# Attention and expert start: layer 0's finish behind the score products, its output product in the turned rows' banks, turned rows copied out in halves, first expert group turned on TensorE

## The chip, the cores and the metric

One core of one Trainium2 chip runs the whole program. The metric is the device time of the program in microseconds (us), median of several runs. The profile is one execution of its own.

## The reference, cut to what matters

```python
x = L0_attn_x                                     # 4 x 2048 x 256, float32
xn = _layernorm(x)
s = _L0_attn_ref(xn, ...)    # tanh recurrence with 16 states; out = H @ Wo.T + bo; out * gate + residual
g = _silu(_L0_ffn_ref(xn, ...))
x = x + s * g
xn = _layernorm(x)
# L1 attention: for each of the 2048 positions i, over the 4 batch entries j <= i ("sequence" is the batch axis),
# 16 heads of 16 columns, softmax_one
q, k, v = (xn @ W.T + b for W, b in ...)          # 256 x 256 each
scores = einsum('ibhd,jbhd->ijbh', q, k) / 4      # causal in i, j
out = einsum('ijbh,jbhd->ibhd', softmax_one(scores, axis=1), v)
# L1 ffn: logits = xn @ wg, top 2 of 8 experts, capacity 2048 rows each;
# relu(rows @ w1[e] + b1[e]) @ w2[e] + b2[e], 256 -> 1024 -> 256, weighted by the gate and summed
x = x + out * _silu(moe(xn))
```

## The kernel before, in words

The program is a chain of stages: `prepare`, `mix` (layer 0 up to its gate and feed-forward, beside the recurrence), `recur` (a repeat of the recurrence that a flag on the chip asks for), `attend`, `experts`, `combine`. Each stage is a block with one instruction list for each engine, written out by hand; engines meet only at semaphores, and each engine takes its own list in order.

`attend` works on 16 tiles t of 128 positions x 4 batch entries. TensorE's list for tile t (L1334 to L1368) is: wait until the turned rows are in SBUF (L1336), the query product into `pY` (bias rows L1357 as matmuls, then L1361), the key product into `pX`, the logits into `pL` (L1348), layer 0's output product of tile t+2 into `pX` (`output`, L1315, behind a wait until the keys have been copied out, L1353), the value product into `pY`, the turning of tile t+1's rows into `pT` (L1325), and the turning of the logits (L1368). Query, key and value products are 16 matmul records each.

VectorE's list for tile t (`body`, L1082) begins with `layer0(t + 2)`: it multiplies layer 0's output product from PSUM with the stored gate (L1043), adds it into `x_st` (L1046), and takes mean and variance (L1051, L1059). Then come the score products, four multiplications of 1024, 768, 512 and 256 columns with both inputs in SBUF (L1090), their sums per head (L1096), the maximum (L1101), the difference (L1104), a wait for ScalarE's exponential (L1271), the sum (L1108), the reciprocal (L1111) and the weights `att` (L1114).

GpSimd (POOL) waits for `att` of tile t, then multiplies weights by values and adds the parts up (L1022, L1028: 1024, then 768 twice, 512 twice, 256 twice). After the first addition it has the four small operations that make scale and shift of tile t+3 (L981 to L989), which wait for L1059 of that tile.

ScalarE's list for tile t (L1289 to L1306) is: exponential of t, keys of t+1 out of PSUM (L1259), the logits' store, the normalisation of tile t+2 (L1235), logits and values of t+1, the turned rows of t+2 (L1259, one copy of 1024 columns), the turned logits of t+1, the queries of t+2.

After the last tile the routing runs on VectorE and TensorE (L1141 to L1212). `experts` then has 32 groups of 512 rows (8 experts of 4 groups). Gathers on POOL's queue (L1535) fetch the rows into `xg`; ScalarE makes the upper half precision part (L1733), VectorE the lower one (L1633), and SyncE turns both with four DMA transposes per group (L1499). TensorE's first layer (L1796 to L1798) has eight units of six matmuls; units 0 and 1 of the next group come ahead of the second layer (L1822 to L1824) of this one. The first expert's w1 is split by L1722 (ScalarE) and L1619 (VectorE) in the stage's start. The bias row of the first expert is a DMA on POOL's queue (L1529). `margin_exp` (L1738) is ScalarE's exponential for the gate.

Of the kernel before, what the change touches and what calls it, by code (L numbers as in the profile page):

```python
# [19 lines left out]
P = 128  # L20
# [753 lines left out]
def recur(nc, v):  # L774

    with ExitStack() as c:
# [4 lines left out]
        with nc.Block() as block:  # L781
# [39 lines left out]
def attend(nc, v):  # L821
# [10 lines left out]
    with ExitStack() as c:  # L832
# [118 lines left out]
        with nc.Block() as block:  # L951
            @block.sync
            def _(sp):
# [11 lines left out]
                sp.wait_ge(t_done, NT)  # L965
# [70 lines left out]
            def _(dve):  # L1036
# [45 lines left out]
                def body(i, u, left):  # L1082
                    t = 2 * i + u
                    if left >= 2:
                        layer0(t + 2)
# [6 lines left out]
                    last.then_inc(sm, 1)  # L1092
                    dve.wait_ge(sm, SM * t + 1)
# [131 lines left out]
            def _(act):  # L1225
# [53 lines left out]
                take(xnT, pT, t_done, t_evac, 0)  # L1279
# [5 lines left out]
                take(xnT, pT, t_done, t_evac, 1)  # L1285
# [3 lines left out]
                def body(i, u, left):  # L1289
# [11 lines left out]
                    if left >= 2:  # L1301
                        take(xnT, pT, t_done, t_evac, t + 2)
# [8 lines left out]
            def _(pe):  # L1311
                def output(t):
                    for n in range(2):
                        half = slice(2 * GRP * n, 2 * GRP * n + 2 * GRP)
                        last = pe.matmul(pX[:, 2 * n:2 * n + 2, :].rearrange("p b d -> p (b d)"),  # L1315
                                         v.h_st[half, :, :][:, t, :],
# [4 lines left out]
                def turn(t, u):  # L1321
# [4 lines left out]
                    last.then_inc(t_done, 1)  # L1326

                output(0)
                pe.wait_ge(op_ready, 1)
                output(1)  # L1330
# [3 lines left out]
                def body(i, u, left):  # L1334
                    t = 2 * i + u
                    pe.wait_ge(t_evac, t + 1)  # L1336
                    for n, (dst, done) in enumerate(((pY, q_done), (pX, k_done), (pY, v_done))):
                        if n == 0:
                            pe.wait_ge(v_evac, t + 1)
                        if n == 1:  # L1340

                            pe.wait_ge(op_ready, t + 2 if left >= 1 else t + 1)
                        if n == 2:
                            if not (isinstance(i, int) and t == 0):
                                pe.wait_ge(l_evac, t)
                            for kk in range(KD):
                                for b in range(B):
                                    last = pe.matmul(pL[GRP * b:GRP * b + GRP, 0:P], v.wgr[:, kk, :],  # L1348
                                                     xnT[:, kk, b * P:(b + 1) * P],
                                                     start=(kk == 0), stop=(kk == KD - 1))  # L1350
                            last.then_inc(l_done, 1)
                            if left >= 2:
                                pe.wait_ge(k_evac, t + 1)  # L1353
                                output(t + 2)
                            pe.wait_ge(q_evac, t + 1)
                        for m in range(2):
                            pe.matmul(dst[:, 2 * m:2 * m + 2, :], ones3[:, :], spread(bias3[:, n * D:(n + 1) * D], 2),  # L1357
                                      start=True, stop=False, skip_group_check=True)
                        for b in range(B):
                            for kk in range(KD):  # L1360
                                last = pe.matmul(dst[:, b, :], xnT[:, kk, b * P:(b + 1) * P],  # L1361
                                                 v.wqkv[:, kk, n * D:(n + 1) * D], start=False, stop=(kk == KD - 1),
                                                 skip_group_check=True)
                        last.then_inc(done, 1)
                    if left >= 1:
                        turn(t + 1, 1 - u)
# [23 lines left out]
def experts(nc, v):  # L1390
# [4 lines left out]
    with ExitStack() as c:  # L1395
# [35 lines left out]
        h_hi = sb("e_h_hi", [P, HT, W], F16)  # L1431
        h_lo = v.free[:, 0:HT * W // 2].bitcast(F16).rearrange("p (h w) -> p h w", h=HT)
# [5 lines left out]
        pY = psum("e_pY", [P, BLK, D])  # L1438

        passed = sem("e_passed")  # L1440
        w1_in, w2_in = v.w1_in, v.w2_in
# [38 lines left out]
        with nc.Block() as block:  # L1480
            @block.sync
            def _(sp):
# [37 lines left out]
                for n in range(2):  # L1520
                    turn(n, n, reused=False)
# [5 lines left out]
            def _(pool):  # L1527

                pool.dma_start(b2b[0], v.eb2[0].partition_broadcast(P)).then_inc(y_out[1], 16)  # L1529
# [9 lines left out]
                for n in range(3):  # L1539
# [21 lines left out]
            def _(dve):  # L1561
# [68 lines left out]
                def x_lower(n):  # L1630
                    dve.wait_ge(x_hi_ready, n + 1)
# [13 lines left out]

                dve.memset(xg[:, :, D + E:], 0.0)
                take_icol(0, 0)
# [254 lines left out]
```

## Time and profile before

| what | value |
|---|---|
| median of 3 runs | 1365.91 us (1365.15 to 1366.03) |
| profiled execution, its own time | 1364.27 us |
| its span, first to last instruction | 1362.5 us |
| busy: PE, DVE, ACT, POOL | 1159.2 (85%), 1003.9 (74%), 623.6 (46%), 613.1 (45%) us |
| mean granted TensorE clock | 0.938 of full |
| attention tiles | first score products at 293.17, last `att` (L1114) ends at 544.3 us |
| experts | first w1 matmul at 624.97, last about 1315 us |

PE is TensorE's matmuls, PEld its weight loads, DVE VectorE, ACT ScalarE, SP SyncE. A row of the timeline begins with its start and its duration in us; the bracket at its end is the time that the engine stood idle before it and what ended that. Rows of one line that follow each other are merged ("x4"). A row of a window table has its bounds, its length, then busy time and count for each engine, then the clock, the share of the DMA engines and GB/s.

### The profile page before, as it was taken

To read this page: it belongs to the slowest core of one execution; us is meant where nothing else is said; L and a number is where in the kernel's file an instruction comes from. 1 tells how busy PE (TensorE), PEld (TensorE's weight loads), DVE (VectorE), ACT (ScalarE), POOL (GpSimd) and SP (SyncE) were. 2 spreads that over 40 slices of the span, in tenths; PEclk is the share of its full clock that TensorE was granted. 3 is DMA by queue.
4 is the path that set the end of the run, shared out by engine and by line. 5 is a ranking of instruction groups with operands and counts; after the bars stand their busy time and mean duration, and the time that the engine had idled before them with its cause. 6 is when DMAs were issued, how large, how long until landed. Compare 5 with 4: busy or idle time off the path is not lost. (4 is left out here: it accounts for less than half of the span.)

```text
span 1362.5 us, 20386 instructions
## 1 busy us (share of the span) xinstructions
PE 1159.2 (85%) x7448; PEld 793.8 (58%) x7448; DVE 1003.9 (74%) x1931; ACT 623.6 (46%) x955; POOL 613.1 (45%) x526
## 2 busy tenths in 40 slices
PE   3799999689989996146999999999999999999920
PEld 3665665267666765133676666766766666667610
DVE  7777777758888889985767677676686766776538
ACT  4865655333443333004545455454455454554422
POOL 5600000028778887213555545645546455463310
PEclk9999999889999998557999999999999999999965
DMA  8170000001111112004645455555555545454259
GB/s 343 61 249 1 1 1 0 1 32 48 33 33 33 33 33 78 1 20 106 118 110 104 83 109 105 114 108 77 113 99 117 111 74 123 90 82 70 32 157 351
DMA packets 142708, 117.61 MB, mean 86 GB/s; under 512 B 83824, under 2 KB 127728, under 8 KB 142480
## 3 DMA queue, kind: packets, MB, share of 16 engines
q1 hardware_dynamic: 109248, 80.75, 19.8%
q0 software_dynamic: 24624, 34.23, 15.9%
q10 hardware_dynamic: 8736, 1.33, 0.5%
q8 instruction: 59, 0.97, 0.3%
q14 instruction: 41, 0.34, 0.1%
HBM read 55.19 MB, written 44.30 MB: 73 GB/s over the span
## 5 line engine op out<-in xcount | busy, mean ns | idle before, releaser
L1758 ACT ACTIVATE e_h_all<-e_pH,e_b1c,e_h_scale 128x512 f32<-128x512 f32 x256 | 199.6, 780 | 258.0 <-PE e_pY L1824 205.5
L1822 PE MATMUL e_pY<-e_w_hi,e_h_hi 128*128 128x256 f16 x1024 | 279.3, 273 | 2.6 <-DVE late L1669 2.6
L1823 PE MATMUL e_pY<-e_w_lo,e_h_hi 128*128 128x256 f16 x1024 | 279.1, 273 | 0.0
L1824 PE MATMUL e_pY<-e_w_hi,late 128*128 128x256 f16 x1024 | 279.1, 273 | 0.0
L1551 POOL DMA_INDIRECT expert_sums<-late,e_dcol x128 | 212.9, 1664 | 103.6 <-DVE late L1709 71.4
L1535 POOL DMA_INDIRECT e_xg<-xn_rows,e_icol x128 | 147.1, 1149 | 240.0 <-DVE e_icol L1567 153.2
L1796 PE MATMUL e_pH<-e_xT,e_w_hi 128*128 128x512 f16 x512 | 194.9, 381 | 15.6 <-DMA e_xT<-e_xs 15.6
L1669 DVE TENSOR_TENSOR late<-e_h_all,e_h_hi 128x512 f16<-128x512 f32 x256 | 177.3, 692 | 36.8 <-ACT e_h_hi L1758 31.1
L1797 PE MATMUL e_pH<-e_xT,e_w_hi 128*128 128x512 f16 x512 | 194.8, 380 | 0.0
L1798 PE MATMUL e_pH<-e_xT,e_w_lo 128*128 128x512 f16 x512 | 194.8, 380 | 0.0
L1705 DVE SCALAR_TENSOR_TENSOR late<-e_pY,e_y_scale,logit_st 128x512 f32<-128x512 f32 x64 | 48.0, 751 | 104.6 <-PE e_pY L1824 100.8
L1361 PE MATMUL c_pY<-late,c_xnT 128*128 128x256 f32 x512 | 117.7, 384 | 0.0
L1822 PEld LDWEIGHTS e_pY<-e_w_hi,e_h_hi 128*128 128x128 f16 x1024 | 100.2, 98 | 19.8 <-DVE late L1669 4.9
L1823 PEld LDWEIGHTS e_pY<-e_w_lo,e_h_hi 128*128 128x128 f16 x1024 | 100.2, 98 | 14.9
L1361 PEld LDWEIGHTS c_pY<-late,c_xnT 128*128 128x128 f32 x512 | 98.8, 193 | 17.0 <-issue 0.3
L1824 PEld LDWEIGHTS e_pY<-e_w_hi,late 128*128 128x128 f16 x1024 | 100.2, 98 | 11.6
L1758 ACT ACTIVATE e_h_hi<-e_pH,e_b1c,e_h_scale 128x512 f16<-128x512 f32 x128 | 99.1, 774 | 0.0
L1796 PEld LDWEIGHTS e_pH<-e_xT,e_w_hi 128*128 128x128 f16 x512 | 50.3, 98 | 73.2 <-DMA e_xT<-e_xs 15.6
L976 POOL MEMSET c_mhalf<- 128x4 f32 x1 | 0.1, 102 | 204.5 <-POOLq L781 204.5
L1798 PEld LDWEIGHTS e_pH<-e_xT,e_w_lo 128*128 128x128 f16 x512 | 50.3, 98 | 60.9 <-issue 1.0
L1797 PEld LDWEIGHTS e_pH<-e_xT,e_w_hi 128*128 128x128 f16 x512 | 50.3, 98 | 56.7 <-issue 0.8
L1028 POOL TENSOR_TENSOR prod_st<-prod_st,c_pv 128x768 f32<-128x768 f32 (+2 forms) x48 | 68.8, 1433 | 8.6 <-POOL c_pv L1022 8.6
(251 smaller groups left out, 2130.0 us busy)
## 6 DMA issues: line engine op xcount, KB each, us to landing
shared<-expert_w SPq DMA_DIRECT2D x16, 1024.0 KB, 6.5
expert_sums<-a_zero SPq DMA_DIRECT2D x10, 1024.0 KB, 11.3
x_st<-x SPq DMA_DIRECT2D x16, 512.0 KB, 9.0
xn_rows<-shared SPq DMA_DIRECT2D x16, 512.0 KB, 3.0
f_ya<-expert_sums SPq DMA_DIRECT2D x16, 512.0 KB, 8.1
out<-x_st SPq DMA_DIRECT2D x8, 1024.0 KB, 8.8
e_xg<-xn_rows,e_icol POOLq DMA_INDIRECT x128
e_xT<-e_xs SPq DMA_TRANSPOSE x128
```

The lines of the kernel that those rows point to most:

```text
L1028: pool.tensor_tensor(o, o, part, ALU.add).then_inc(pv_step, 1)
L1361: last = pe.matmul(dst[:, b, :], xnT[:, kk, b * P:(b + 1) * P], v.wqkv[:, kk, n * D:(n + 1) * D], start=False, stop=(kk == KD - 1), skip_g ...
L1535: pool.indirect_dma_start(xg[:, q, 0:D + E], None, v.xn3_dram, bass.IndirectOffsetOnAxis(icol[u][:, q:q + 1], axis=0), bounds_check=N - 1, ...
L1551: pool.indirect_dma_start(v.y_dram, bass.IndirectOffsetOnAxis(dcol[u][:, q:q + 1], axis=0), yo[:, q, :], None, bounds_check=N + CAP - 1, o ...
L1669: dve.tensor_tensor(h_lo[:, h, :], h_all[h % 2][:, :], h_hi[:, h, :], ALU.subtract).then_inc(h_lo_ready, 1)
L1758: last = act.activation(dst, pH[h % NPH][:, :], ACT.Relu, bias=b1c[eu][:, h:h + 1], scale=h_scale[eu][:, 0:1])
L1796: pe.matmul(pH[h % NPH][:, :], w1_hi[:, k, rows], x_hi[:, k, :], start=(k == 0), stop=False)
L1797: pe.matmul(pH[h % NPH][:, :], w1_hi[:, k, rows], x_lo[:, k, :], start=False, stop=False)
L1798: last = pe.matmul(pH[h % NPH][:, :], w1_lo[:, k, rows], x_hi[:, k, :], start=False, stop=(k == KD - 1))
L1822: pe.matmul(pY[:, q, :], h_hi[:, h, cols], w2_hi[:, h, :], start=(h == 0), stop=False)
L1823: pe.matmul(pY[:, q, :], h_hi[:, h, cols], w2_lo[:, h, :], start=False, stop=False)
L1824: last = pe.matmul(pY[:, q, :], h_lo[:, h, cols], w2_hi[:, h, :], start=False, stop=(h == HT - 1))
```

## The change

It has three places. In `recur`, ScalarE's wait within the conditional repeat is one lower. In `attend`, `layer0(t + 2)` moves from the head of VectorE's tile to behind the score products; its output product moves from behind the logits to between query and key product and goes into `pT`, so the turning of the next tile's rows waits until L1043 has read it; the turned rows are copied out in two halves of 512 columns, the query product starts its first half after the first of them, and its bias matmuls are ahead of that wait. In `experts`, the gathers of the first group go ahead of the bias row's DMA, its rows are split in four parts, turned on TensorE into PSUM and copied out by ScalarE, in place of four DMA transposes; VectorE splits w1 after that; and ScalarE's `margin_exp` of a group moves one group later.

```diff
@@ recur, ScalarE
-                        act.wait_ge(summed, L * n + l + 1)
+                        act.wait_ge(summed, L * n + l)
@@ attend, VectorE
                 def layer0(t):
                     dve.wait_ge(o_done, t + 1)
-                    dve.tensor_tensor(v.prod_st[:, t, :], pX[:, :, :].rearrange("p b d -> p (b d)"),
-                                      v.prod_st[:, t, :], ALU.mult).then_inc(op_ready, 1)
+                    src = pX[:, :, :].rearrange("p b d -> p (b d)") if t < 2 else pT[:, :, :].rearrange("p k c -> p (k c)")
+                    dve.tensor_tensor(v.prod_st[:, t, :], src, v.prod_st[:, t, :], ALU.mult).then_inc(op_ready, 1)
...
                 def body(i, u, left):
                     t = 2 * i + u
-                    if left >= 2:
-                        layer0(t + 2)
                     dve.wait_ge(k_evac, t + 1)
                     dve.wait_ge(q_evac, t + 1)
...
                     last.then_inc(sm, 1)
+                    if left >= 2:
+                        layer0(t + 2)
                     dve.wait_ge(sm, SM * t + 1)
@@ attend, ScalarE (in the place of take(xnT, pT, ...))
+                def take_turned(t):
+                    for kk in range(KD):
+                        act.wait_ge(t_done, KD * t + kk + 1)
+                        act.activation(xnT[:, kk, :], pT[:, kk, :], ACT.Copy).then_inc(t_evac, 1)
@@ attend, TensorE (turn now signals t_done after each kk)
+                def product(t, n, dst, done):
+                    for m in range(2):
+                        pe.matmul(dst[:, 2 * m:2 * m + 2, :], ones3[:, :], spread(bias3[:, n * D:(n + 1) * D], 2),
+                                  start=True, stop=False, skip_group_check=True)
+                    for kk in range(KD):
+                        if n == 0:
+                            pe.wait_ge(t_evac, KD * t + kk + 1)
+                        for b in range(B):
+                            last = pe.matmul(dst[:, b, :], xnT[:, kk, b * P:(b + 1) * P], ...)
+                    last.then_inc(done, 1)
...
                 def body(i, u, left):
                     t = 2 * i + u
+                    pe.wait_ge(v_evac, t + 1)
+                    product(t, 0, pY, q_done)
+                    if left >= 2:
+                        output(t + 2, in_pT)
+                    if t == 0:
+                        pe.wait_ge(op_ready, 2)
+                    else:
+                        pe.wait_ge(k_evac, t)
+                    product(t, 1, pX, k_done)
...
+                    last.then_inc(l_done, 1)
+                    pe.wait_ge(q_evac, t + 1)
+                    product(t, 2, pY, v_done)
                     if left >= 1:
+                        if left >= 2:
+                            pe.wait_ge(op_ready, t + 3)
                         turn(t + 1, 1 - u)
@@ experts, SyncE and POOL
-                for n in range(2):
-                    turn(n, n, reused=False)
+                sp.wait_ge(first_turned, BLK)
+                turn(1, 1, reused=False)
...
-                pool.dma_start(b2b[0], v.eb2[0].partition_broadcast(P)).then_inc(y_out[1], 16)
+                pool.wait_ge(icols, 1)
+                for q in range(BLK):
+                    pool.indirect_dma_start(xg[:, q, 0:D + E], None, v.xn3_dram, ...).then_inc(first_in[q], 16)
+                pool.dma_start(b2b[0], v.eb2[0].partition_broadcast(P)).then_inc(y_out[1], 16)
+                for n in range(1, 3):
                     gather(n, n % 2)
@@ experts, VectorE
                 scales(0, 0)
-                lower_w1(0, 0)
-                x_lower(0)
+                for q in range(BLK):
+                    dve.wait_ge(first_hi, q + 1)
+                    last = dve.scalar_tensor_tensor(xs[:, q, D:2 * D], ...).then_inc(first_lo, 1)
+                dve.sem_inc(x_lo_ready, 1)
+                for q in range(BLK):
+                    dve.wait_ge(first_in[q], 16)
                 margin(0, 0, 0)
                 take_icol(1, 1)
+                lower_w1(0, 0)
                 x_lower(1)
@@ experts, ScalarE
+                act.activation(ident16, v.ident, ACT.Copy).then_inc(ident_ready, 1)
+                for q in range(BLK):
+                    act.wait_ge(first_in[q], 16)
+                    act.activation(xs[:, q, 0:D], xg[:, q, 0:D], ACT.Copy, scale=X_SCALE).then_inc(first_hi, 1)
                 upper_w1(0, 0)
-                x_upper(0, 0, 1)
+                for q in range(BLK):
+                    cols = slice(q * P, (q + 1) * P)
+                    act.wait_ge(first_turned, q + 1)
+                    act.activation(xT[0][:, :, cols], first_turn[q], ACT.Copy).then_inc(first_ready, 1)
                 margin_exp(0, 0)
                 x_upper(1, 1, 1)
-                margin_exp(1, 1)
...
-                        margin_exp(n + 2, (g + 2) % GRPS)
+                        margin_exp(n + 1, (g + 1) % GRPS)
@@ experts, TensorE
+                pe.wait_ge(ident_ready, 1)
+                for q in range(BLK):
+                    pe.wait_ge(first_lo, q + 1)
+                    for kk in range(2 * KD):
+                        last = pe.transpose(first_turn[q][:, kk, :], xs[:, q, kk * P:(kk + 1) * P], ident16)
+                    last.then_inc(first_turned, 1)
+                pe.wait_ge(first_ready, BLK)
+                pe.sem_inc(x_turned, 16 * BLK)
```

## Rows read from the trace of the kernel before

**Rows 1.** Busy time of each engine in three stretches (window table).
```profile
368.90:499.40 130.50, 116.99 (x666) 90.15 (x666) 114.73 (x185) 52.95 (x89) 104.91 (x88) 1.00 0.11 34
...
603.00:625.00 22.00, 0.98 (x4) 0.61 (x5) 10.58 (x22) 3.16 (x3) 8.92 (x9) 0.50 0.38 80
625.00:1315.00 690.00, 674.04 (x4629) 452.65 (x4629) 472.60 (x923) 343.35 (x518) 351.93 (x248) 0.99 0.51 95
```
**Rows 2.** Waits, 320 to 499 us: total, times, longest.
```profile
DVE prod_st L1043 <- PE c_pX L1315: 10.6, 11, 1.3
```
**Rows 3.** Timeline of one attention tile in the steady state, 352 to 369 us.
```profile
352.44 1.13 PE L1315 MATMUL c_pX<-late,shared 64*128 64x512 f32 x4 [0.54 <-ACT c_work L1259]
352.71 1.93 POOL L1022 TENSOR_TENSOR prod_st<-c_att,c_v 128x1024 f32<-128x1024 f32 x1 [1.70 <-DVE c_att L1114]
...
354.82 1.49 POOL L1022 TENSOR_TENSOR c_pv<-c_att,c_v 128x768 f32<-128x768 f32 x1 [0.18 <-POOL prod_st L1022]
354.87 2.52 DVE L1046 TENSOR_TENSOR x_st<-prod_st,x_st 128x1024 f32<-128x1024 f32 x1
356.49 2.58 POOL L1028 TENSOR_TENSOR prod_st<-prod_st,c_pv 128x768 f32<-128x768 f32 x1 [0.18 <-POOL c_pv L1022]
...
357.39 1.04 PE L1325 MATMUL c_pT<-cst,shared 128*128 128x128 f32 x8
...
359.50 2.99 DVE L1090 TENSOR_TENSOR c_work<-c_work 128x1024 f32<-128x1024 f32 x4
...
360.10 3.62 PE L1361 MATMUL c_pY<-late,c_xnT 128*128 128x256 f32 x16
...
362.53 3.00 DVE L1096 TENSOR_REDUCE c_sc<-c_work 128x64 f32<-128x1024 f32 x4
...
363.98 3.62 PE L1361 MATMUL c_pX<-late,c_xnT 128*128 128x256 f32 x16
...
368.69 0.42 DVE L1114 TENSOR_TENSOR c_att<-c_ex,c_mx 128x256 f32<-128x256 f32 x1
```
**Rows 4.** Timeline, tile 14: no layer 0 work is left, so score products follow `att`.
```profile
515.82 7.67 DVE L1090 TENSOR_TENSOR c_work<-c_work 128x1024 f32<-128x1024 f32 x4
...
529.69 0.42 DVE L1114 TENSOR_TENSOR c_att<-c_ex,c_mx 128x256 f32<-128x256 f32 x1
```
**Rows 5.** Timeline, tile 0 and what leads to it.
```profile
278.49 0.20 POOL L981 TENSOR_TENSOR c_ta<-c_mv,c_eps 128x4 f32<-128x4 f32 x1 [7.93 <-DVE c_mv L1059]
...
286.33 1.02 ACT L1259 ACTIVATE c_work<-c_pX 128x1024 f32<-128x1024 f32 x1 [2.86 <-PE c_pX L1361]
...
288.59 1.22 DVE L1043 TENSOR_TENSOR prod_st<-c_pX,prod_st 128x1024 f32<-128x1024 f32 x1 [10.18 <-PE c_pX L1315]
...
293.17 3.00 DVE L1090 TENSOR_TENSOR c_work<-c_work 128x1024 f32<-128x1024 f32 x4
```
**Rows 6.** Groups by line, 150 to 600 us: a 512-column copy out of PSUM.
```profile
L667 ACT ACTIVATE a_gT<-a_pGU,gconst 128x512 f32<-128x512 f32 x9 | 6.2, 687 | 6.2 <-PE a_pGU L750 6.2
```
**Rows 7.** Timeline, the start of the experts, 611 to 640 us.
```profile
611.22 2.00 ACT L1722 ACTIVATE e_w_hi<-shared,e_scale 128x2048 f16<-128x2048 f32 x1 [68.68 <-DVEq L1615]
...
616.85 15.96 SPq L1499 DMA_TRANSPOSE e_xT<-e_xs  x8
...
624.97 0.61 PE L1796 MATMUL e_pH<-e_xT,e_w_hi 128*128 128x512 f16 x1 [15.55 <-DMA e_xT<-e_xs]
...
625.16 1.06 ACT L1733 ACTIVATE e_xs<-e_xg 128x1024 f16<-128x1024 f32 x1 [7.56 <-DMA e_xg<-xn_rows,e_icol]
...
639.88 0.27 PE L1822 MATMUL e_pY<-e_w_hi,e_h_hi 128*128 128x256 f16 x1
```
**Rows 8.** TensorE at its lower clock: a query product (timeline), and a fall (window table).
```profile
276.83 5.58 PE L1361 MATMUL c_pY<-late,c_xnT 128*128 128x256 f32 x16
...
533.60:536.00 2.40, 0.03 (x1) 0.00 (x0) 2.40 (x3) 1.11 (x2) 2.22 (x2) 1.00 0.00 0
536.00:537.00 1.00, 0.00 (x0) 0.00 (x0) 1.00 (x1) 0.00 (x0) 1.00 (x1) 0.90 0.00 0
```

More of the change, by code:

```diff
@@ L1278, in _ @@
                 normalise(0, 0, 0)
-                take(xnT, pT, t_done, t_evac, 0)
+                take_turned(0)
                 normalise(1, 1, 0)
@@ L1284, in _ @@
                 take_v(0, 0, reused=False)
-                take(xnT, pT, t_done, t_evac, 1)
+                take_turned(1)
                 put_logits(0)
@@ L1301, in body @@
                     if left >= 2:
-                        take(xnT, pT, t_done, t_evac, t + 2)
+                        take_turned(t + 2)
                     if left >= 1:
@@ L1311, in _, with output @@
             def _(pe):
-                def output(t):
+                def output(t, dst):
                     for n in range(2):
                         half = slice(2 * GRP * n, 2 * GRP * n + 2 * GRP)
-                        last = pe.matmul(pX[:, 2 * n:2 * n + 2, :].rearrange("p b d -> p (b d)"),
-                                         v.h_st[half, :, :][:, t, :],
+                        last = pe.matmul(dst[n], v.h_st[half, :, :][:, t, :],
                                          v.wo_pad[half, 2 * n:2 * n + 2, :].rearrange("p b d -> p (b d)"),
@@ L1325, in turn @@
                             last = pe.transpose(pT[:, kk, b * P:(b + 1) * P], xn[u][:, b, kk * P:(kk + 1) * P], ident)
-                    last.then_inc(t_done, 1)
-                output(0)
+                        last.then_inc(t_done, 1)
+                def product(t, n, dst, done):
[6 more added lines that the diff above has]
+                        for b in range(B):
+                            last = pe.matmul(dst[:, b, :], xnT[:, kk, b * P:(b + 1) * P],
+                                             v.wqkv[:, kk, n * D:(n + 1) * D], start=False, stop=(kk == KD - 1),
+                                             skip_group_check=True)
+                    last.then_inc(done, 1)
+                in_pX = [pX[:, 2 * n:2 * n + 2, :].rearrange("p b d -> p (b d)") for n in range(2)]
+                in_pT = [pT[:, n, :] for n in range(2)]
+                output(0, in_pX)
                 pe.wait_ge(op_ready, 1)
-                output(1)
+                output(1, in_pX)
                 turn(0, 0)
@@ L1335, in body @@
                     t = 2 * i + u
[L1336 to L1358, printed above, removed]
-                        for b in range(B):
[L1360 to L1364, printed above, removed]
@@ new lines, in body @@
+                    pe.wait_ge(v_evac, t + 1)
[7 more added lines that the diff above has]
+                    product(t, 1, pX, k_done)
+                    if t:
+                        pe.wait_ge(l_evac, t)
+                    for kk in range(KD):
+                        for b in range(B):
+                            last = pe.matmul(pL[GRP * b:GRP * b + GRP, 0:P], v.wgr[:, kk, :],
+                                             xnT[:, kk, b * P:(b + 1) * P], start=(kk == 0), stop=(kk == KD - 1))
@@ L1438, in experts @@
         pY = psum("e_pY", [P, BLK, D])
+        first_turn = [pH[q][:, 0:KD * P].bitcast(F16).rearrange("p (k w) -> p k w", k=2 * KD) for q in range(BLK)]
         passed = sem("e_passed")
+        first_in = [sem(f"e_first_in{n}") for n in range(BLK)]
+        ident_ready = sem("e_ident_ready")
+        first_hi = sem("e_first_hi")
+        first_lo = sem("e_first_lo")
+        first_turned = sem("e_first_turned")
+        first_ready = sem("e_first_ready")
         w1_in, w2_in = v.w1_in, v.w2_in
@@ L1537, in gather @@
                                                 bounds_check=N - 1, oob_is_err=False).then_inc(x_in[u], 16)
-                for n in range(3):
+                pool.wait_ge(icols, 1)
+                for q in range(BLK):
+                    pool.indirect_dma_start(xg[:, q, 0:D + E], None, v.xn3_dram,
+                                            bass.IndirectOffsetOnAxis(icol[0][:, q:q + 1], axis=0),
+                                            bounds_check=N - 1, oob_is_err=False).then_inc(first_in[q], 16)
+                pool.dma_start(b2b[0], v.eb2[0].partition_broadcast(P)).then_inc(y_out[1], 16)
+                for n in range(1, 3):
                     gather(n, n % 2)
```

16 lines of the change are left out of this document (9 added, 7 removed).

## The prediction

> **What bounds the kernel now.** I read the window table first. In eight steady attention tiles (130.5 us, 16.3 each) TensorE is busy 117 us and VectorE 115, POOL 105: nobody has much room, and the period is set by a ring of all of them [rows 1]. In the experts TensorE is busy 674 of 690 us, so there only an earlier start can pay; in the 22 us before, it is busy 1 [rows 1]. The waits show what the attention part of the change goes for: VectorE stands 10.6 us in 11 tiles for layer 0's output product, about 0.97 each [rows 2], and TensorE stands 0.54 us for the keys' copy ahead of it [rows 3].
>
> The timeline of one tile shows what the sums below rest on. VectorE and POOL get in each other's way when both work out of SBUF: L1046 took 2.52 us, from 354.87 to 357.39, beside a POOL multiplication that ended at 356.31, and the POOL addition issued at 356.49 ended at 359.07, 1.68 after L1046 did [rows 3]. Alone L1046 takes what L1043 takes, 1.22. The four score products took 2.99, because in this order they meet only POOL's small operations [rows 3]. In tile 14 there is no layer 0 work left; the score products follow `att` at once, as POOL begins its three large operations, and the same four instructions took 7.67 us [rows 4]. That is the order which the change makes the rule for tiles 1 to 13.
>
> **The attention, part by part.** Let S be the start of a tile's score products and D their length. Two rings must close.
>
> VectorE's ring: D, then layer 0 work, 4.6 (288.59 to 293.17, undisturbed, since POOL then waits for its statistics [rows 5]), then sums to the end of `att`, 6.6 (362.53 to 369.11 [rows 3]): from the products' end to the end of `att` 11.2. Then a pause d until the next keys are there. Period = d + D + 11.2.
>
> TensorE's ring, new: the turning now waits for L1043, which waits for the score products. After D: L1043 1.27 with its gap; the first half turned, about 0.9 (eight transposes 1.04 plus their load [rows 3]); its copy 0.6, between half of the 1.02 for 1024 columns [rows 5] and the 0.69 of a 512-column one [rows 6]; 0.3 to the first matmul; query start to key start 3.88 (360.10 to 363.98, the keys' bias in it) [rows 3]; the output product in between 1.1 [rows 3]; key product 3.62 [rows 3]; keys' copy 1.02 with 0.03 of gap [rows 5]. Sum 12.7. Period = D + 12.7. Logits, value product and the value copy lie beside VectorE's D + 1.3 and cost nothing; if D were 3.0 they would stick out by about half a microsecond. The query bias now lies in that shadow too. The second half's copy is behind the first four matmul pairs, nothing. Normalisation, exponential and stores on ScalarE keep their order; it is free when the halves come.
>
> The two rings give d = 12.7 - 11.2 = 1.5. Now D, from the end of `att`: POOL's first product runs 0.1 to 2.0 (1.93 [rows 3]); score product 1 waits for it and ends at 3.2; POOL's second (1.49) to 4.7; product 2 to 5.6; the addition (1.68) to 7.3; products 3 and 4 to 8.2. So D = 8.2 - 1.5 = 6.7, by taking turns as in tile 14, where 2.99 + 1.93 + 1.49 + 1.68 = 8.1 stands against 7.67 measured, the last product's end tucked in; I take 6.6 [rows 3, 4]. **Period 6.6 + 12.7 = 19.3 us, against 16.3.** Lower bound: no pause, D = 7.67 and VectorE's ring alone, 18.9. Upper bound: POOL comes late. It must wait for the statistics until 4.6 after the score products and has 13.1 busy a tile [rows 1], 5.1 of it done: it would end at 12.6, 1.4 after `att`, and D would grow to 8.1, period 20.8. But its small operations are short when VectorE holds nothing: L981 took 0.20 [rows 5] where it meets score products now, so I expect it ready about when `att` is.
>
> What goes away, 0.97 of wait for the output product and about 0.7 of L1046's mean delay, is in these rings already.
>
> The Trainium skill, page "SBUF — State Buffer", section "Who interferes with whom", says that a VectorE instruction with two SBUF inputs and a GpSimd instruction that reads SBUF shut each other out for a whole instruction. By that rule the eight pieces can only follow each other, 8.1 from the end of `att`; it doesn't say who is next when one of VectorE's ends and POOL waits, and if VectorE were, the period would be that of the first rival below. The row of tile 14 speaks for turns.
>
> First tile: the keys' copy ended at 287.35 [rows 5]. The query product starts some 1.5 to 2 earlier, and the output product ahead of the keys costs about 2 at the low clock of that stretch [rows 8], so S(0) = 287.5. POOL is idle then, D = 3.0, so S(1) = 287.5 + 3.0 + 12.7 = 303.2. Thirteen periods: S(14) = 303.2 + 13 x 19.3 = 554.1, against 515.82 [rows 4]: +38.3. Tiles 14 and 15 keep their order; D there falls from 7.67 to about 6.6 in two tiles but the key chain sets most of it: -1.2. **Attention +37.1** (bounds: 18.9 gives 32, 20.8 gives 57). The copy's added fixed cost, 16 times 0.2 to 0.3, is on ScalarE, which has over half its time free [rows 1].
>
> **Recurrence.** The wait stands in a conditional; no instruction of L810 is in this trace. Zero, unless the repeat ran.
>
> **Start of the experts.** Scales are done at 611.2, when L1722 starts [rows 7]. First group new: gathers are issued from about 603.3 instead of 604.3 and land by 611; ScalarE's four small parts are done by then; VectorE's four lower parts take 1.3 to 1.7, to 612.8; TensorE turns, to 613.4; ScalarE has w1 until 613.2, then four copies of 512 columns at about 0.66, to 616.0; VectorE splits w1 until 615.8. First matmul at 616.1 instead of 624.97 [rows 7]: 8.9 earlier. But group 1 still comes by DMA: its gather starts about 3.8 earlier than before (L1567 moves ahead of the w1 split), so ScalarE's part comes at about 621.3 for 625.16, the lower part ends near 623.7, and the four transposes take what they took, 8.1 (616.85 to 624.97) [rows 7]: 631.9. TensorE needs them at about 628.5 and stands some 3 us, and ScalarE can't empty the first banks before 622.4, which is hidden behind four banks. Second layer at 634.5 for 639.88 [rows 7]. **-5.4**, kept to the end since TensorE is full from there; bounds -3 (slower transposes) and -8.9 (no stall). Dropping one DMA issue on POOL ahead of the gathers, four transposes on SyncE's queue, and the moved `margin_exp`: ScalarE isn't what TensorE waits for, nothing.
>
> **Sum.** +37.1 - 5.4 = +31.7 on the profiled execution: 1364.3 + 31.7 = 1396.0. The median of the runs is 1.6 above that execution; I predict 1397.
>
> **Rivals.**
> 1. *VectorE keeps its turn* (faster). Once it has begun, its four products run together, D = 0.5 + 3.0 = 3.5, period 16.2: the attention ends where it did, -1 with the first tile, the experts give 5.4: 1359. It decides in the four products after `att`; if D stays under about 4 the kernel is faster. Against it: 7.67 in tile 14, no reason to think that tile special [rows 4]. 8%. A milder form, D near 4.5, ends within 0.2% to 1% above; with it 2% for no change.
> 2. *TensorE's clock falls in its new gap* (slower still). From the value product's end, S + 3.8, to the turning, S + 7.9, it stands about 4.1 us. After its last matmul of the attention (to 533.63) the clock was full until 536.0 and 0.90 on the mean of the next microsecond, so it fell at about 536.8, 3.2 us on; the query product took 5.58 there for 3.62 [rows 8, 3]. The Trainium skill, page "TensorE: Matmul & The Clock Gate", section "Why this matters for your kernels", warns that such gaps between bursts send the clock back; by that rule this case would come in part of the tiles. The price is small, since a later key copy makes d longer and lets POOL finish first: with 2.2 more in TensorE's ring d is 3.7, D 4.9, period 19.8; with 4.4 more, 20.1. 13 times 0.5 to 0.8, and perhaps 2 in the expert start: 1404 to 1409. 20%.
> 3. *POOL late*, D = 8.1: period 20.8, 1397 + 19.5 = 1416. 8%.
>
> The forecast itself, 62%, has 1388 to 1403 as its own range. The whole range 1383 to 1415 leaves out rival 1, most of rival 3 and a little of each side. 0.2% (2.7 us) is about what a measurement of this kernel can tell from no change. Faster 0.09, same 0.02, slower 0.89.
>
> **What would show it.** Right: L1090's group near 6.5 us a tile in place of 3.6, L1046 at 1.23 in all tiles, `att` every 19.3 us, a TensorE wait of about 4 us for L1043 ahead of L1325, VectorE's wait for L1315 gone, a new one of 1.5 for the keys' copy. In the experts the first L1796 11.9 us or so after the first gather's index copy, then a stall of 3 on the transposes. Wrong: L1090 at 3 to 4 us, or a period under 17.

## The result, and the profile after

| | before | after |
|---|---|---|
| median of 4 runs, side by side | 1365.53 us (1364.99 to 1366.03) | 1402.72 us (1402.48 to 1404.19) |
| span of the profiled execution | 1362.5 us | 1401.0 us |
| mean granted TensorE clock | 0.938 | 0.930 |

The ratio is 1.0275, with a 95% interval of 1.0257 to 1.0292: 37 us slower. Forecast were 1397 us and a range of 1383 to 1415. The sign, the mechanism and the range held; the point was 5.7 us too low.

From the profile page of after, the busy time of each engine:

```profile
PE 1179.9 (84%) x7464; PEld 805.3 (57%) x7464; DVE 1031.3 (74%) x1934; ACT 626.4 (45%) x979; POOL 586.3 (42%) x526
```

The work is the same but for 16 more matmuls (the first group's turning, x7464 for x7448), and TensorE is busy 20.7 us longer with it: a first sign that it ran at the lower clock more often. VectorE is busy 27.4 us longer, since the time that an instruction of VectorE stands behind one of POOL counts as busy. POOL is busy 26.8 us less: its small operations for the statistics (L981 to L987), which had lain beside the score products and took 3.2 us a tile before, now take 1.4.

**Where the 38.5 us of span went.** The stages ahead of the attention end 0.46 us later. The last `att` ends at 584.77 instead of 544.31, so the attention takes 40.0 more. The routing behind it takes the same (58.68 and 58.71 from there to the first gather's index copy). From that copy to the table load of `combine`, 709.58 for 711.51: 1.9 less. 0.46 + 40.0 - 1.9 = 38.5.

The waits of after, 325 to 540 us (engine, line, released by; total, times, longest), show what the tile is made of now.

```profile
POOL c_ta L981 <- DVE c_mv L1059: 67.9, 11, 6.4
...
PE c_pT L1329 <- DVE prod_st L1044: 40.1, 11, 4.6
...
DVE c_work L1088 <- ACT c_work L1259: 23.0, 11, 2.6
```

The wait that the change went for, VectorE's 0.97 a tile for the output product [rows 2], is gone. In its place VectorE waits 2.1 a tile for the keys (L1088), and TensorE 3.6 a tile for L1044 ahead of the turning. Both are the new waits that were forecast. POOL waits 6.2 a tile for statistics, but in time: it starts each tile's first large operation 0.5 after `att` starts, as before, so rival 3 did not come.

The timeline of after over one tile and the start of the next two (start, duration; in the bracket the idle time ahead and what ended it) holds the whole ring. D is again the time of a tile's four score products.

```profile
359.37 0.42 DVE L1114 TENSOR_TENSOR c_att<-c_ex,c_mx 128x256 f32<-128x256 f32 x1
359.87 1.93 POOL L1022 TENSOR_TENSOR prod_st<-c_att,c_v 128x1024 f32<-128x1024 f32 x1 [0.89 <-DVE c_att L1114]
...
361.35 1.02 ACT L1259 ACTIVATE c_work<-c_pX 128x1024 f32<-128x1024 f32 x1 [3.34 <-PE c_pX L1340]
...
361.98 1.49 POOL L1022 TENSOR_TENSOR c_pv<-c_att,c_v 128x768 f32<-128x768 f32 x1 [0.18 <-POOL prod_st L1022]
...
362.41 5.57 DVE L1088 TENSOR_TENSOR c_work<-c_work 128x1024 f32<-128x1024 f32 x4 [2.61 <-ACT c_work L1259]
363.66 2.57 POOL L1028 TENSOR_TENSOR prod_st<-prod_st,c_pv 128x768 f32<-128x768 f32 x1 [0.18 <-POOL c_pv L1022]
...
367.90 1.21 DVE L1044 TENSOR_TENSOR prod_st<-c_pT,prod_st 128x1024 f32<-128x1024 f32 x1
369.15 1.23 DVE L1046 TENSOR_TENSOR x_st<-prod_st,x_st 128x1024 f32<-128x1024 f32 x1
...
369.17 1.09 PE L1329 MATMUL c_pT<-cst,shared 128*128 128x128 f32 x8 [3.29 <-DVE prod_st L1044]
...
370.64 3.62 PE L1340 MATMUL c_pY<-late,c_xnT 128*128 128x256 f32 x16
...
374.18 1.13 PE L1320 MATMUL c_pT<-late,shared 64*128 64x512 f32 x4
...
375.69 3.62 PE L1340 MATMUL c_pX<-late,c_xnT 128*128 128x256 f32 x16
...
379.05 0.42 DVE L1114 TENSOR_TENSOR c_att<-c_ex,c_mx 128x256 f32<-128x256 f32 x1
...
379.34 1.02 ACT L1259 ACTIVATE c_work<-c_pX 128x1024 f32<-128x1024 f32 x1 [1.66 <-PE c_pX L1340]
...
380.40 6.88 DVE L1088 TENSOR_TENSOR c_work<-c_work 128x1024 f32<-128x1024 f32 x4 [0.92 <-ACT c_work L1259]
...
388.47 1.97 PE L1329 MATMUL c_pT<-cst,shared 128*128 128x128 f32 x8 [4.60 <-DVE prod_st L1044]
...
401.01 5.95 DVE L1088 TENSOR_TENSOR c_work<-c_work 128x1024 f32<-128x1024 f32 x4 [2.24 <-ACT c_work L1259]
```

Read it from 362.41. The score products take 5.57 and 6.88 where they took 2.99 [rows 3], because POOL's three large operations lie among them. L1046 takes 1.23 where it took 2.52 [rows 3]. From the products' end (367.98) the chain L1044, turning, query product, output product, key product, copy (379.34) leads to the next products at 380.40: 12.42, where 12.7 was forecast. 12.42 and D = 6.88 make 19.30, and the next `att` does start at 398.35, 19.30 after 379.05.

The second turn of the ring differs. The turning at 388.47 took 1.97 instead of 1.09, after a wait of 4.60. The window table of after for two microseconds around it (busy time and count of PE, PEld, DVE, ACT, POOL, then the clock):

```profile
387.00:388.00 1.00, 0.00 (x0) 0.00 (x0) 1.00 (x2) 0.00 (x0) 0.00 (x0) 0.89 0.00 0
388.00:389.00 1.00, 0.53 (x3) 0.53 (x4) 0.96 (x2) 0.00 (x0) 0.00 (x0) 0.50 0.00 0
```

TensorE stood from 383.87 on, and the granted clock went from full to half, 2.4 to 1.2 GHz, at about 387.8. From the products' end (387.28) to the next ones (401.01) it is then 13.73: 1.31 more. VectorE starts its products later, meets less of POOL (D 5.95 for 6.88), and the `att` after that comes 19.67 instead of 19.30 later. So a fall costs 0.37 of period. By the starts of L1114 and L1088 in this trace, the chain took 12.42 in 4 of the 13 transitions between tiles 0 and 13 (periods 19.29 to 19.30) and 13.7 to 14.1 in the other 9 (19.67 to 19.69, one 19.86).

Two more things stand in the record of the granted clock. A tenth fall lies in tile 13, behind the last of these transitions. And the length of TensorE's wait does not decide alone: with the same 3.3 us, tiles 4, 8 and 12 kept the full clock, and tiles 7 and 11 lost it.

The start of the experts in after (timeline). "SPq" is SyncE's queue.

```profile
643.45 0.17 DVE L1590 COPY e_icol<-late 128x4 int32<-128x4 int32 x1 [0.81 <-PEq L951]
...
654.05 2.35 DVE L1642 SCALAR_TENSOR_TENSOR e_w_lo<-shared,e_scale,e_w_hi 128x2048 f16<-128x2048 f32 x1 [0.36 <-ACT e_w_hi L1751]
654.57 2.76 POOL L1552 DMA_INDIRECT e_xg<-xn_rows,e_icol  x1 [4.11 <-DVE e_icol L1590]
...
656.65 0.58 PE L1838 MATMUL e_pH<-e_xT,e_w_hi 128*128 128x512 f16 x1 [2.56 <-DVE e_w_lo L1642]
...
657.63 0.99 POOL L1552 DMA_INDIRECT e_xg<-xn_rows,e_icol  x1 [0.30 <-issue]
...
663.06 1.06 ACT L1761 ACTIVATE e_xs<-e_xg 128x1024 f16<-128x1024 f32 x1 [7.01 <-DMA e_xg<-xn_rows,e_icol]
...
665.58 5.23 SPq L1518 DMA_TRANSPOSE e_xT<-e_xs  x4
...
678.67 0.27 PE L1864 MATMUL e_pY<-e_w_hi,e_h_hi 128*128 128x256 f16 x1
```

The first w1 matmul comes 13.20 after the index copy; it came 21.95 after it before (603.02 to 624.97 [rows 7]): 8.75 earlier. The second layer begins 35.22 after the copy for 36.86: only 1.64 earlier. Between lie a wait of 1.46 for ScalarE, which was busy with group 1's upper half, and one of 3.31 for group 1's transposes, until 674.38. Behind that the clock was low once more, until about 677.9: 0.68 of full on the mean of 676 to 679 us. From the end of the wait for the transposes to the second layer it is 4.29.

### The profile page after: what moved, and what is told of

It is laid out like the page before. It is cut to its first block and busy times, and to the rows that moved or that the text cites. A ratio compares the mean times of both kernels' runs of the same rounds, so it can differ in the third digit from the quotient of the medians.

```text
span 1401.0 us, 20442 instructions
## 1 busy us (share of the span) xinstructions
PE 1179.9 (84%) x7464; PEld 805.3 (57%) x7464; DVE 1031.3 (74%) x1934; ACT 626.4 (45%) x979; POOL 586.3 (42%) x526
## 5 line engine op out<-in xcount | busy, mean ns | idle before, releaser
L1552 POOL DMA_INDIRECT e_xg<-xn_rows,e_icol x124 | 140.5, 1133 | 241.6 <-DVE e_icol L1590 141.2
L1088 DVE TENSOR_TENSOR c_work<-c_work 128x1024 f32<-128x1024 f32 (+1 forms) x64 | 96.5, 1565 | 36.0 <-ACT c_work L1259 36.0
L1340 PE MATMUL c_pY<-late,c_xnT 128*128 128x256 f32 x512 | 122.0, 393 | 0.0
L1340 PEld LDWEIGHTS c_pY<-late,c_xnT 128*128 128x128 f32 x512 | 103.1, 202 | 20.6 <-issue 2.5
```

What stands on the lines that cost most here:

```text
L1088: last = dve.tensor_tensor(qk[:, PAIR0[j]:PAIR0[j] + w, :], q[:, j:B, :], spread(k[:, j, :], w), ALU.mult)
L1552: pool.indirect_dma_start(xg[:, q, 0:D + E], None, v.xn3_dram, bass.IndirectOffsetOnAxis(icol[u][:, q:q + 1], axis=0), bounds_check=N - 1, ...
```

## The experiments

The kernel before, beside them, had medians of 1364.96 (e1 to e4) and 1364.97 us (e5 to e8).

**e1: the order undone, all else kept.**

```diff
                 def body(i, u, left):
                     t = 2 * i + u
+                    if left >= 2:
+                        layer0(t + 2)
                     dve.wait_ge(k_evac, t + 1)
...
-                    if left >= 2:
-                        layer0(t + 2)
                     dve.wait_ge(sm, SM * t + 1)
```

> The changed kernel with one thing undone: layer0(t + 2) is back ahead of the score products on VectorE. The output product in the turned rows' banks, the two halves and the new expert start stay. Theory (the score products beside POOL's three large operations are the loss): L1090's group goes back to 3.0 to 4.1 us a tile, L1044 no longer waits for its product since that is made before the keys, the turning waits for nothing, and the period is 15.0 to 15.6 us; 1350 to 1354 us in all. Rival (the wait of the turning for L1044 or the place of the output product is the loss): the period stays above 17 and the kernel above 1375.

Measured: 1352.58 us (1351.15 to 1353.06), ratio 0.9907 (0.9891 to 0.9924). Timeline of e1:

```profile
458.94 0.42 DVE L1114 TENSOR_TENSOR c_att<-c_ex,c_mx 128x256 f32<-128x256 f32 x1
...
463.98 1.81 POOL L1028 TENSOR_TENSOR prod_st<-prod_st,c_pv 128x768 f32<-128x768 f32 x1 [0.18 <-POOL c_pv L1022]
464.55 4.13 DVE L1090 TENSOR_TENSOR c_work<-c_work 128x1024 f32<-128x1024 f32 x4
...
474.87 0.42 DVE L1114 TENSOR_TENSOR c_att<-c_ex,c_mx 128x256 f32<-128x256 f32 x1
```

The period is 15.93. The products no longer wait for keys; the first of them meets the end of POOL's third operation, and they take 4.13. The bound is VectorE itself, and it is a little slower than expected. One move in VectorE's list is thus worth 50.1 us of after, and e1 is faster than both kernels: with the old order the rest of the change pays.

**e4: the order alone, in the kernel before.** The same move as in the change, and nothing else.

```diff
-                    if left >= 2:
-                        layer0(t + 2)
                     dve.wait_ge(k_evac, t + 1)
...
                     last.then_inc(sm, 1)
+                    if left >= 2:
+                        layer0(t + 2)
```

> The kernel before with only layer0(t + 2) moved behind the score products on VectorE; product into pX, whole copies and expert start as before. Theory: VectorE's ring alone, no pause for the keys, score products 7.67, period 18.9 to 19.4; 1398 to 1406 us. Rival (the loss needs the turned rows' banks to be shared): period 16.3, 1366.

Measured: 1399.37 us (1398.22 to 1399.98), ratio 1.0250 (1.0233 to 1.0267): +34.4. Timeline of e4:

```profile
455.08 0.42 DVE L1114 TENSOR_TENSOR c_att<-c_ex,c_mx 128x256 f32<-128x256 f32 x1
455.42 7.68 DVE L1088 TENSOR_TENSOR c_work<-c_work 128x1024 f32<-128x1024 f32 x4
455.58 2.84 POOL L1022 TENSOR_TENSOR prod_st<-c_att,c_v 128x1024 f32<-128x1024 f32 x1 [0.89 <-DVE c_att L1114]
...
460.78 2.05 POOL L1028 TENSOR_TENSOR prod_st<-prod_st,c_pv 128x768 f32<-128x768 f32 x1 [0.18 <-POOL c_pv L1022]
...
474.17 0.42 DVE L1114 TENSOR_TENSOR c_att<-c_ex,c_mx 128x256 f32<-128x256 f32 x1
```

and its groups by line and shape, 362 to 530 us:

```profile
L1088 DVE TENSOR_TENSOR c_work<-c_work 128x768 f32<-128x768 f32 x9 | 24.2, 2687 | 0.0
L1088 DVE TENSOR_TENSOR c_work<-c_work 128x256 f32<-128x256 f32 x9 | 18.3, 2029 | 0.0
...
L1088 DVE TENSOR_TENSOR c_work<-c_work 128x1024 f32<-128x1024 f32 x8 | 9.7, 1218 | 0.0
```

Here VectorE is first: its 1024-column product runs free in 1.22, and POOL's first large operation takes 2.84 for 1.93. Then each of the three smaller products costs 2.0 to 2.7 (the one of 512 columns 1.98), though the one of 256 columns is the smallest piece of work among them: each stands behind one POOL operation. That is taking turns, one instruction each. D is the 7.68 of tile 14 [rows 4], and no pause for keys follows, which is the lower bound of the forecast (18.9): 19.09 here. The order by itself costs nearly all that the change loses. In this trace the granted clock fell in six tiles of the attention too, and the period stayed at 19.1: where VectorE sets the ring, the fall costs nothing that shows.

**e2: the attention alone, with the expert start of before.** The function `experts` is that of the kernel before.

> The changed attention with the expert start of before. Theory: the attention costs 40 us and the expert start gives back about 2, so 1404.5 to 1405. Rival: the new expert start gives the 5 that was forecast and the attention costs more elsewhere: 1408.

Measured: 1405.73 us (1404.72 to 1406.76), ratio 1.0301 (1.0283 to 1.0318). That is 0.7 above the expected range and 2.3 below the rival. The attention costs 40.8 over before; beside the 1402.72 of after the expert start is worth 3.0. Against e4, the shared banks and TensorE's new order cost a further 6.4 once VectorE's order is moved. With the old order the same edits gain 8.8 (e1 against e5, below).

**e5: the expert start alone, in the kernel before.**

> The kernel before with the new expert start alone. Theory (read from the changed kernel's trace: first w1 matmul 8.7 us earlier against the index copy, then 3.3 us of wait for the second group's transposes and 1.7 us at the lower clock behind it, and 1.5 us until ScalarE is free): 2 us are left, 1362.5 to 1364. Rival (the start gives its 5): 1360 or less.

Measured: 1361.41 us (1360.50 to 1362.60, 8 runs), ratio 0.9975 (0.9964 to 0.9985): 3.6 faster. That is more than I expected after reading the trace of after, and less than the 5.4 of the prediction; it lies between the theory and the rival. A window of e5:

```profile
627.00:629.00 2.00, 2.00 (x6) 0.76 (x5) 1.97 (x5) 2.00 (x5) 1.50 (x2) 0.50 0.61 121
```

The clock fell a second time in e5 as well, but ahead of the stall (about 626.5 to 630) and not behind it. TensorE ran dry later, its wait for group 1's transposes is 1.77, and the second layer begins 2.60 after that wait for the 4.29 of after. Over the whole stage, index copy to table load, the traces of five kernels with this expert start (after, e1, e5, e6, e7) gave 706.9 to 709.6 us and those of before, e2 and e4 711.5 to 712.4. The first group scatters by about as much as the start is worth, so I go by the runs: 3.0 and 3.6. The scatter can be read. The transposes are there 29.9 to 30.9 us after the index copy, and the second layer begins 2.6 us later in e5, e6 and e7, but 3.9 in e1 and 4.3 in after, the two whose clock fell behind the stall.

**e3: POOL's three large operations cut to one head.**

```diff
+                        hs = slice(0, 1) if j < 2 else slice(0, H)
-                        pool.tensor_tensor(part.rearrange("p (i h d) -> p i h d", i=w, h=H), a, row,
+                        pool.tensor_tensor(part.rearrange("p (i h d) -> p i h d", i=w, h=H)[:, :, hs, :],
+                                           a[:, :, hs, :], row[:, :, hs, :],
                                            ALU.mult).then_inc(pv_step, 1)
...
+                            cs = slice(0, DK) if j == 1 else slice(0, (B - j) * D)
-                            pool.tensor_tensor(o, o, part, ALU.add).then_inc(pv_step, 1)
+                            pool.tensor_tensor(o[:, cs], o[:, cs], part[:, cs], ALU.add).then_inc(pv_step, 1)
```

> The changed kernel with POOL's first three large operations of a tile cut to one head of 16 columns per entry (the weighted values of heads 1 to 15 for the first two entries are left out). All waits stay. Theory (mutual exclusion of VectorE and POOL): the score products take 3.0 to 3.6 us, TensorE's ring closes at 12.5 + 3.1 = 15.6, the kernel takes 1346 to 1352. Rival (the new dependency of the turning on L1044 makes the period by itself): the period stays above 18 us, 1385 or more.

Measured: 1341.08 us (two runs, 1340.40 and 1341.75), ratio 0.9825 (0.9806 to 0.9845). Timeline of e3:

```profile
456.38 0.43 DVE L1116 TENSOR_TENSOR c_att<-c_ex,c_mx 128x256 f32<-128x256 f32 x1
...
456.88 0.30 POOL L1023 TENSOR_TENSOR prod_st<-c_att,c_v 128x64 f32<-128x64 f32 x1 [0.90 <-DVE c_att L1116]
...
457.73 3.05 DVE L1090 TENSOR_TENSOR c_work<-c_work 128x1024 f32<-128x1024 f32 x4 [0.93 <-ACT c_work L1261]
...
471.83 0.42 DVE L1116 TENSOR_TENSOR c_att<-c_ex,c_mx 128x256 f32<-128x256 f32 x1
```

VectorE's order is that of after, and still D is 3.05 and the period 15.45. TensorE's wait for the turning shrinks to 0.77, and the clock stays full in all these tiles. So it is not the place of layer 0's finish as such, nor TensorE's longer chain, that costs the time: it is that the score products now meet POOL's large operations. Less POOL work behind the last tile is in this time too, so it came out below the expected span of 1346 to 1352.

**e6: the gap of TensorE filled.** Twelve matmuls into a bank that nobody uses, ahead of the wait for L1044.

```diff
                         if left >= 2:
+                            for m in range(12):
+                                pe.matmul(pR[:, :], ones3[:, :], spread(bias3[:, 0:D], 2), start=True, stop=True)
                             pe.wait_ge(op_ready, t + 3)
```

> The changed kernel with twelve extra matmuls a tile (bias rows into a bank that nothing reads) in TensorE's gap ahead of its wait for L1044. Theory: the gap falls to about 1 to 2 us, the granted clock stays full in the attention, TensorE's ring is 12.4 behind the score products in every tile, the period is 19.2 to 19.3 instead of 19.6 on the mean, and the kernel takes 1397 to 1399. Rival (the clock has no price here): within 1.5 us of the changed kernel's 1402.7. A second one (extra matmuls are in the way): above 1405.

Measured: 1400.16 us (1399.37 to 1401.28), ratio 1.0261 (1.0246 to 1.0277): 2.6 less than after, outside the theory and outside both rivals; the interval overlaps that of after. Timeline of e6, one tile where the clock held and one where it did not:

```profile
467.45 1.09 PE L1329 MATMUL c_pT<-cst,shared 128*128 128x128 f32 x8 [2.02 <-DVE prod_st L1044]
...
481.99 2.75 PE L1377 MATMUL d_pR<-c_bias,c_ones 128*128 128x512 bf16 x12
...
486.76 1.97 PE L1329 MATMUL c_pT<-cst,shared 128*128 128x128 f32 x8 [2.02 <-DVE prod_st L1044]
```

Of the nine falls in the 13 transitions three are left, and the periods without one are 19.30 to 19.32, but for one of 19.95. But the total does not prove the price. Six falls less give 6 x 0.37 = 2.2; the filling made tile 0 1.6 later (its wait was only 0.75 there) and that one tile 0.6 longer; `att` of tile 13 starts at 554.97, for 554.99 in after. The tenth fall of after, in tile 13, is gone as well: VectorE no longer waits 1.26 for the keys ahead of tile 14's products, and the last `att` starts 0.9 earlier. The rest of this trace's gain lies in the expert stage (706.9 for 709.6), where the two kernels have the same code: the transposes were there 1.1 earlier, and no fall followed them. What a fall costs is better read tile by tile: 19.67 for 19.30 in after, and 19.69 for 19.31 in e6's own three. Why the clock still fell in three tiles, after waits of only 2.02, stays open.

**e7: e1 with the turned rows copied out in one piece.**

```diff
-                    for kk in range(KD):
-                        act.wait_ge(t_done, KD * t + kk + 1)
-                        act.activation(xnT[:, kk, :], pT[:, kk, :], ACT.Copy).then_inc(t_evac, 1)
+                    act.wait_ge(t_done, KD * t + KD)
+                    act.activation(xnT[:, :, :], pT[:, :, :], ACT.Copy).then_inc(t_evac, KD)
```

> The kernel with layer0's place restored (e1), and the turned rows copied out in one piece of 1024 columns instead of two halves. Theory: there VectorE's ring sets the period of 15.9 us and TensorE has room, so the halves are worth nothing: within 1.5 us of e1's 1352.6. Rival (TensorE's ring sets the period in e1): 16 tiles x 0.4 us, 1359.

Measured: 1353.62 us (1351.53 to 1356.18), ratio 0.9919 (0.9904 to 0.9934), against 0.9907 of e1. The intervals overlap: where VectorE is the bound, the halves are worth nothing that these runs can tell. In after, where TensorE's chain counts, they were not tried apart.

**e8: e1 without the early units ahead of the first second layer.** An attempt to lift the stall on group 1's transposes.

```diff
                     if g == 0:
                         pe.wait_ge(w1_lo_ready, e + 1)
                         pe.sem_inc(passed, 1)
+                    if g == 0 or n == 1:
                         first_layer(e, g, n, range(EARLY))
                     first_layer(e, g, n, range(EARLY, HT))
-                    if g < GRPS - 1:
+                    if g < GRPS - 1 and n > 0:
                         first_layer(e, g + 1, n + 1, range(EARLY))
```

> The kernel with layer0's place restored (e1), and in the first expert group alone the second layer is not preceded by two units of the next group, so TensorE doesn't stand for the second group's transposes. Theory: the wait of 3.3 us and the lower clock behind it go, the second layer's start then waits for VectorE's split of w2; 1.5 to 3 us less than e1: 1349.5 to 1351. Rival (VectorE sets the end of that stretch anyway): within 0.7 us of e1.

Measured: 1355.84 us (1354.24 to 1356.04), ratio 0.9929 (0.9915 to 0.9942): 3.3 slower than e1, where a gain was expected. The intervals of the two ratios overlap a little, so the loss is less sure than the missing gain. The theory fell. The waits of TensorE in e8, 615 to 660 us, and a window of it:

```profile
PE e_pY L1865 <- DVE e_w_lo L1649: 3.0, 3, 1.1
```

```profile
631.00:633.00 2.00, 2.00 (x11) 1.40 (x10) 0.86 (x8) 0.00 (x0) 0.51 (x1) 0.50 0.36 75
```

and of e1 after its own stall:

```profile
629.00:631.00 2.00, 2.00 (x21) 1.80 (x19) 1.86 (x7) 0.01 (x1) 0.00 (x0) 1.00 0.02 4
```

The second layer did begin earlier (622.59 for 628.00), but w2's lower half was not ready: VectorE was still splitting it, and TensorE stood three times. The clock fell and stayed at half for 6.8 us (from about 627.6 to 634.4); in e1 it was low for 3.4, until 628.9. The last piece of w2's split ends 33.1 after the index copy in e1 and in e8 alike, and e1's second layer begins only at 33.8: the stall on the transposes had hidden the split.

## Why the prediction was right, and where it was off

**The score products meet POOL's large operations: right.** D was put at 6.6, against 3.5 for rival 1. Measured: 5.57 to 6.88 in after, 3.05 in e3 without POOL's work, 7.68 in e4. By the Trainium skill, page "SBUF — State Buffer", section "Who interferes with whom", the two engines shut each other out for whole instructions; the trace agrees, with 7.81 and 8.19 from one `att`'s end to the end of the next products, beside the 8.2 of the forecast (four products and three POOL operations, so seven pieces where the prediction says eight). That VectorE doesn't keep its turn is settled by e4's shapes; rival 1 is out.

**The ring: right in its sum, off in its shares.** VectorE's part from products to `att` was put at 11.2 and is 11.49: L1104 takes 1.12 in after (0.66 before), since POOL's 256-column operations now lie beside it. It costs nothing, as TensorE's chain is the longer one and the pause d shrinks to 0.92 (forecast 1.5). TensorE's chain, put at 12.7, is 12.42; D is 6.88. 12.42 + 6.88 = 19.30, the forecast period to the digit, wherever the clock holds.

**The attention's size: the step that failed is the choice between my own case and rival 2.** I gave the clock's fall 20% and left it out of the sum. It came in 9 of 13 transitions. The ring then grew by 1.3 to 1.7, less than the 2.2 that the rival took, and the period by 0.37, less than its 0.5. The damping is as argued there: later keys let POOL finish first. In us: tile 1's products start at 302.47 for 303.2, -0.7; the 13 periods took 254.2 for 250.9, +3.3; tiles 14 and 15 gained 0.4 and not 1.2, +0.8. 37.1 - 0.7 + 3.3 + 0.8 = 40.5, the measured difference at the last `att`, of which 0.46 lies ahead of the stage. The clock accounts for both pluses, as an estimate: nine falls at 0.37 are 3.3, and the tenth, in tile 13, is worth the 0.9 by which e6 ends the attention earlier without it. The warning of the Trainium skill, page "TensorE: Matmul & The Clock Gate", section "Why this matters for your kernels", which the prediction weighed, agrees with this trace in that the falls came with the new gaps; but not every gap of that length brought one, and e6 had three after waits of 2.02. What misled me was one row, a fall 3.2 us after the last matmul of the attention [rows 8]: I took 4.1 us of gap as near that and still unlikely to matter. In after the fall came in waits of 3.3 to 4.6, and in some tiles only after the turning had begun.

**Rival 3, POOL late: did not come.** POOL had its statistics in time and was ready at `att` in every steady tile.

**Recurrence: zero, as forecast.** The routing and the stages ahead moved by less than 0.5.

**Start of the experts: right at the first matmul, mis-sized behind it.** The first w1 matmul came 13.20 after the index copy; my times (616.1 for 603.02) make it 13.1. (The "11.9" of the prediction's last part does not agree with that sum; 13.1 is the number.) The term that failed is the arrival of group 1's transposes, put at 631.9, that is 28.9 after the copy; it was 30.9 (671.07, when TensorE ran dry, plus 3.31). 1.4 of that are already in the lower part, which ended 22.05 after the copy for 20.7, and 0.7 in the transposes themselves (8.9 for 8.2). Ahead of it the first gather of group 1 took 2.76 on POOL where the next took 0.99. That is 2.0 of the miss. The other 1.7 is a second fall of the clock after the stall, which I had put at nothing: 4.29 from the transposes to the second layer, for the 2.6 of my times (634.5 - 631.9), which e5, e6 and e7 do show. The wait of 1.46 for ScalarE is a third thing that I had wrong, as I had written that four banks hide it; but it cost nothing here, since TensorE had to stand for the transposes anyway. 5.4 - 2.0 - 1.7 = 1.7. So 8.75 were won at the first matmul, 1.64 were left at the second layer, and by the runs the start is worth 3.0 to 3.6 for 5.4.

Together: +40.0 + 0.46 - 1.9 = 38.5 on the profiled execution against +31.7. The median of after lies at its profiled execution, so the 1.6 by which the median of before lay above its own was not there a second time. 1396.0 + 1.6 would be 1397.6; the point was put at 1397, 1.0 above 1396.0, and so it missed by 5.7 and not by 6.8.

**What pays.** The change as a whole loses because of one of its moves. With `layer0(t + 2)` left at the head of VectorE's tile, the rest (the output product in the turned rows' banks, the copy in halves, the new expert start) is 12.4 us faster than before.

## What to carry to other kernels

When two engines exclude each other at SBUF, an order is not only about who waits for whom by semaphore: ask which long instructions of the other engine each group will lie beside, and add the two up instead of laying them over each other. Before a wait is moved, look in the trace for a place where the new neighbourhood already exists (here the last tiles, 7.67 for 2.99) and take its price. And where a move opens a gap of several microseconds on TensorE in every tile, put the lower clock into the sum and not among the risks, at the price that the ring pays: 0.37 us a tile here where TensorE's chain closes the ring, nothing that shows in e4 where VectorE does.

## What the runs showed of the hardware that I had not expected

- The exchange at the shared SBUF access is one for one even where the pieces are very unequal: in e4 a 256-column product took 2.03 us and a 768-column one 2.69, each beside one POOL operation; alone they are around 0.4 and 0.9 (411 and 945 ns in e1). The same values come back in every tile from 3 to 13 of e4 (D 7.68 each time). That it is a fixed turn and not chance is inferred from that, and no run tests the rule of the exchange itself.
- The issue of a gather on POOL took 2.76 us (after, at 654.57) and 2.73 (e1, at 605.31) while VectorE split w1; the median of all 128 gathers is 1.03 in both traces. The trace of after repeats it: a gather was issued beside the w1 split of each of the other seven experts as well, took 2.31 to 2.32 us every time, and ended 0.96 after the split did. So the gather seems to wait for the split's end; no run took the split away.
- The clock can fall after the work has resumed. In the tile from 427.82 in after the turning ran at full clock, and the query product behind it took 4.78:

```profile
427.00:428.00 1.00, 0.18 (x2) 0.18 (x3) 0.96 (x2) 0.00 (x0) 0.00 (x0) 1.00 0.00 0
428.00:429.00 1.00, 1.00 (x10) 0.94 (x10) 1.00 (x1) 0.49 (x1) 0.00 (x0) 0.87 0.00 0
429.00:430.00 1.00, 1.00 (x4) 0.64 (x3) 0.86 (x4) 0.69 (x3) 0.00 (x0) 0.50 0.00 0
```

- A fall of the clock in a ring that another engine shares cost 0.37 us a tile, though TensorE's own chain grew by 1.3 to 1.7.
